# Layer 3's slots: the front's pieces in other steps of a batch

## What is computed

```python
# attention branch, heads of 8 channels
q, k, v = split(x @ qkv_w.T + qkv_b)
k, v = layernorm(k), layernorm(v)              # over the 8 channels of a head
kv = einsum('bhqd,bhqe->bhde', k, v) / Q * temperature + attn_bias
att = einsum('bhqd,bhde->bhqe', q, kv) + x
y1 = gelu(att @ p1_w.T + p1_b) @ p2_w.T + p2_b + x
# feed-forward branch, soft mixture of 16 experts with 64 slots each
x = layernorm(x); se = layernorm(slot_embeds) * scale
logits = einsum('bnd,esd->bnes', x, se)
dispatch = softmax(logits, axis=1)             # over the tokens
slots = einsum('bnd,bnes->besd', x, dispatch)
```

## Time and profile before

| what | value |
|---|---|
| median of 3 runs | 2108.69 us (2106.41 to 2111.24) |
| the profiled execution, in all | 2109.77 us |
| its span | 2107.9 us |
| mean granted TensorE clock | 0.965 |
| TensorE matmul busy, whole span | 1911.7 us (91%) |
| VectorE / ScalarE / GpSimd busy | 1685.2 (80%) / 1469.3 (70%) / 1214.1 us (58%) |
| stage of the slots | about 1674 to 1895 us |

### The profile page before, as it was taken

The page is one execution under the profiler, slowest core; times in us unless marked ns, Lnnn a source line. Parts: engine busy times, 40 slices in busy tenths (PEclk is TensorE's granted clock), DMA queues, the critical chain, the costliest instruction groups (busy, mean ns, idle before and its releaser), DMA issues.

```text
span 2107.9 us, 38803 instructions
## 1 busy us (share of the span) xinstructions
PE 1911.7 (91%) x13494; PEld 1464.8 (69%) x13494; DVE 1685.2 (80%) x3903; ACT 1469.3 (70%) x2914; POOL 1214.1 (58%) x1026
## 2 busy tenths in 40 slices
PE   4899999999999998687986999999999888889998
PEld 3667676767667676554683888888887666668797
DVE  7899999989898998377197888888888787764686
ACT  5788888888878788154235767777777777776575
POOL 3878888787878875167062555555555554437300
PEclk7999999999999999599998999999999999999999
DMA  6999898899989884201000000000001000012000
GB/s 189 340 311 319 287 321 282 312 306 310 313 286 319 285 300 172 91 1 39 1 1 6 1 1 1 1 1 1 1 1 32 0 1 1 1 34 87 11 2 41
DMA packets 72264, 263.99 MB, mean 125 GB/s; under 512 B 10822, under 2 KB 30406, under 8 KB 71558
## 3 DMA queue, kind: packets, MB, share of 16 engines
q1 hardware_dynamic: 71126, 256.53, 35.8%
q10 hardware_dynamic: 944, 4.98, 0.6%
HBM read 140.17 MB, written 121.31 MB: 124 GB/s over the span
## 4 chain that ended last, share of the span: by engine, by line
PE 41%; ACT 7%; DVE 6%; POOL 1%; issue 1%; DVEq 0%; ACTq 0%; POOLq 0%
PE PS L157 11%; PE PS L161 8%; PE PS L335 8%; PE PS L163 8%; PE PS L162 7%; ACT AR L167 3%; ACT L167 1%; DVE DR L181 1%; DVE AR L185 1%; ACT PT L171 1%; DVE PT L181 1%; POOL AR L176 1%; DVE AR L181 1%; DVE AR L193 1%; ACT AR L171 1%
## 5 line engine op out<-in xcount | busy, mean ns | idle before, releaser
L167 ACT ACTIVATE AR<-PS,AR 128x512 f32<-128x512 f32 x1024 | 697.7, 689 | 213.5 <-DVE AR L193 105.4
L193 DVE TENSOR_REDUCE AR<-PS 128x1 f32<-128x512 f32 x896 | 615.2, 687 | 92.5 <-PE PS L163 77.3
L335 PE MATMUL PS<-ident,AR 128*128 128x128 f32 x3816 | 582.0, 277 | 30.0 <-DVE PT L181 15.0
L157 PE MATMUL PS<-AR 128*128 128x128 bf16 (+7 forms) x4126 | 488.7, 358 | 53.1 <-DVE AR L1375 14.2
L335 PEld LDWEIGHTS PS<-ident,AR 128*128 128x128 f32 x3816 | 444.0, 142 | 123.7 <-issue 42.9
L181 POOL TENSOR_TENSOR AR<-AR 128x512 f32<-128x512 f32 (+6 forms) x325 | 389.1, 1216 | 208.0 <-DVE AR L181 91.4
L176 POOL TENSOR_SCALAR AR<-AR 128x512 f32<-128x512 f32 (+1 forms) x146 | 252.8, 1732 | 272.3 <-DVE AR L1743 203.7
L171 ACT ACTIVATE AR<-PS 128x512 f32<-128x512 f32 (+3 forms) x596 | 346.6, 586 | 80.5 <-PE PS L335 46.4
L157 PEld LDWEIGHTS PS<-AR 128*128 128x128 bf16 (+4 forms) x4126 | 290.9, 131 | 134.5 <-issue 61.7
L171 ACT ACTIVATE PT<-PS 128x512 fp32r<-128x512 f32 x320 | 191.3, 598 | 165.1 <-PE PS L335 130.5
L181 DVE TENSOR_TENSOR AR<-PS,AR 128x512 f32<-128x512 f32 (+3 forms) x321 | 211.5, 659 | 69.9 <-PE PS L157 58.0
(11 more groups left out here) (175 smaller groups left out, 2958.8 us busy)
## 6 DMA issues: line engine op xcount, KB each, us to landing
scr<-AR SPq DMA_DIRECT2D x128, 800.0 KB, 4.4
XN<-scr SPq DMA_DIRECT2D x85, 768.0 KB, 6.4
AR<-scr SPq DMA_DIRECT2D x43, 768.0 KB, 6.5
AR<-qsc SPq DMA_DIRECT2D x96, 192.0 KB
qsc<-AR SPq DMA_DIRECT2D x16, 384.0 KB, 4.0
qsc<-AR SPq DMA_DIRECT2D x16, 256.0 KB, 4.5
AR<-in_wgu SPq DMA_DIRECT2D x16, 256.0 KB, 3.1
qsc<-AR SPq DMA_DIRECT2D x16, 128.0 KB, 3.9
```

The lines of the kernel that those rows point to most:

```text
L157: return pe.e.matmul(out, lhsT, rhs, start=start, stop=stop)
L167: return ac.e.activation(out, in_, func, bias=bias, scale=scale, accum_out=accum)
L193: return dv.e.tensor_reduce(out, in_, AX.X, ALU.max, negate=True)
L335: return pe.e.transpose(out, in_, ident[0:k, 0:k])
```

## The change

Only the four tables of steps change. Their values become tuples, so that a step may hold two pieces of one entry, and `in_order` reads them so. The inputs' tables (I_PE, I_DV, I_AC, I_PO) stay.

```diff
-        F_PE = {1: "tr", 3: "kv0", 4: "q", 5: "kv1", 13: "km", 15: "kq", 23: "p1", 26: "p2"}
-        F_DV = {2: "z", 4: "kv0", 6: "kv1", 8: "v1", 10: "vn", 14: "km", 16: "ta", 27: "x2"}
-        F_AC = {2: "hi", 5: "qt", 7: "sq", 9: "root", 10: "xnh", 24: "gelu"}
+        F_PE = {2: ("tr",), 4: ("kv0",), 6: ("q", "kv1"), 16: ("km",), 20: ("kq",), 23: ("p1",), 26: ("p2",)}
+        F_DV = {3: ("z",), 5: ("kv0",), 7: ("kv1",), 10: ("v1",), 12: ("vn",), 17: ("km",), 21: ("ta",), 27: ("x2",)}
+        F_AC = {3: ("hi",), 7: ("qt",), 9: ("sq",), 11: ("root",), 12: ("xnh",), 24: ("gelu",)}
         AMID = ("qt", "root")
-        F_PO = {3: "lo", 5: "pb", 11: "gb", 13: "polo"}
+        F_PO = {5: ("lo",), 7: ("pb",), 12: ("gb",), 14: ("polo",)}
...
-            at = {u: [(pieces[u - 8 * b], b) for b in range(NB) if u - 8 * b in pieces] + ([(inputs[u], 0)] if u in inputs else [])
+            at = {u: [(what, b) for b in range(NB) for what in pieces.get(u - 8 * b, ())] + ([(inputs[u], 0)] if u in inputs else [])
                   for u in range(-PRE3, STEPS3)}
```

## The result

The changed kernel takes 2139.39 us (median; 2138.69 to 2140.00) against 2109.97 us for the kernel before on the same chip: ratio 1.0136, 95% interval 1.0121 to 1.0151, so 29.4 us slower. The forecast was 2128.0 us, slower, with a range of 2110 to 2138. The result lies 1.4 us above that range. The direction and the wait that carried the forecast were right; the size was short by some 10 us, most of what the runs can account for being a cost of TensorE's clock that the forecast put at nothing.

What follows compares the result with a forecast made beforehand. Bound: ScalarE's 13.4 us block, `z` and `lo`, then four TensorE steps. Start-up 1.0, five batches 16.7, last batch 0.4 and drain 1.2 sum to 19.3 us, taking 2108.69 to 2128.0 us; range 2110 to 2138.

Steps and rivals of the forecast that it cites:

- One load more per batch, six times: ScalarE: 4 table loads a batch instead of 3, in 6 batches, 7.7 us of ScalarE; whether it shows depends on place.
- Step 3: TensorE's pv waits for ScalarE's slot copy behind the root, starting 6.15 us after step 2's last matmul (R); idle 5.0 us.
- Step 6: TensorE starts at 14.3 instead of 12.4 after R, as GpSimd's gb holds up VectorE's `norm`: 1.9 us.
- The batch: One batch of layer 3's slots takes 29.75 us instead of 26.42: 3.33 more, five times 16.7.
- Steps 7 and 2: TensorE's small waits: 0.5 us before step 7's pv, 0.6 us before step 2's scores, for ScalarE.
- The clock: TensorE at half clock for about 3.2 us on steps 4 to 5 behind the idle; counted as 0, hidden by VectorE's chain.
- The rival: Slower still by the clock: half clock not hidden, 1.6 us a batch, 8 in all, total 2140; chance 0.13.
- Start-up: Stretch before the first full batch: u = 24 starts 0.3 us later, 1 us with the held `norm` of u = 21; counted 1.0.
- Drain: End of the stage behind the last batch: 1.2 us more; the experts' later weight transfer costs nothing.
- The table serves both: Rival: the logarithm's table also serves exp, step 3 is 2.56 shorter, batch 27.2 us, 2115; chance 0.14 with the side-waits rival.
- Faster: Rival: splitting ScalarE's block frees TensorE; batch 25 us, 2102, or 2087 with all waits hidden; chance 0.07.
- No change: the side waits vanish: Rival: gb's hold, the qt and the exp load hide; batch 26.4 us, 2111; chance 0.14 with the table rival.

Runs made afterwards that it cites:

- e5: Changed kernel with the root in step 5 (r = 13) instead of step 3, vn and gb at 14, km at 17 and 18: 2100.39 us, ratio 0.9946.
- e1: Changed kernel with ScalarE's slot copy issued right behind step 3's `hi`, ahead of the root: 2139.57 us, ratio 1.0135.
- e9: Changed kernel with 40 extra transposes of the identity on TensorE ahead of the pv that waits behind the root: 2133.87 us, ratio 1.0103.
- e11: The kernel before, unchanged, profiled and timed once more: 2111.70 us, ratio 1.0003.
- e8: The changed kernel, unaltered, profiled and timed a second time: 2139.40 us, ratio 1.0132.
- e10: Changed kernel with entry 0's front pieces left in the steps of the kernel before, entries 1 to 7 as changed: 2136.34 us, ratio 1.0111.
- e2: Changed kernel with the root's logarithm replaced by an exponential, so no table load is left in the root: 2113.64 us, ratio 1.0014.
- e6: Kernel before with only the k-and-v chain (root, vn, gb, km, kq and others) moved, inputs and projections left: 2108.82 us, ratio 0.9988.

## Why the prediction was right and where it fell short

- **One load more per batch, six times:** right. From 1674 us on there are 31 loads instead of 25. Worked out as a cost it was rightly not counted by itself: e5 has the same 31 and is faster than the kernel before.
- **Step 3, the step that carried the forecast:** right to 0.1 us (pv at R + 6.25 for 6.15, wait 4.60 for 5.0). e1 confirms that `lo` for the next transposes is late by the same amount. The reading of the earlier trace rows was loose: of the 14.0 us only 12.3 stand before the scores (five waits of 2.46), the rest before pv.
- **Step 6:** right. At full clock (e9) it starts at R + 14.36 for 14.3, waiting 1.78 us for 1.9, and `norm` takes 1.53 us under gb. VectorE and GpSimd, the changed kernel:

```profile
1808.70 1.53 DVE L176 TENSOR_SCALAR AR<-AR 128x512 f32<-128x512 f32 x1
```

```profile
1807.60 4.90 POOL L181 TENSOR_TENSOR AR<-AR 128x1024 f32<-128x1024 f32 x2 [14.14 <-DVE AR L181]
```

  The Trainium skill's "SBUF — State Buffer" (SBUF: two separate sides) has whichever of the two engines starts first hold the shared port pair for its whole instruction. These rows agree, as do the 2.12 us of the start-up and the 2.37 of the last batch: each of these `norm`s ends 0.3 us behind the end of the gb instruction in which it was issued (1810.23 here, against 1807.60 + 2.35).
- **The batch:** 29.94 us at full clock for a forecast of 29.75. The 26.42 from which it was subtracted is not at full clock, though: it is the mean over four batches of 26.43 to 26.58, with 3.4 us at half clock in each, and one of 26.04 without. The earlier trace rows are all from that one. In e11 too the one batch at 1.00 takes 26.04, the others 26.34 to 26.57. At full clock on both sides the change costs 3.9 us a batch, not 3.5. Steps 7 and 2 have the small waits that the text gave them (0.19 and 0.30 for 0.5; 0.31 for 0.6).
- **The clock, the step that failed:** "I take 0 of it, as VectorE's chain to step 6 is 1.9 us longer than TensorE's". The cover was real and of that size (1.78), but the stretch at half clock was sized from one behind an idle of 2.5 us (put at 3.2 us, by the reading above 3.4) and is 6.8 us behind 4.6 in eight of the ten batches of the two profiles. The five batches pay 1.1 us for it in the first profile (150.81 less e9's 149.72) and 3.3 in the second (153.06). The last batch was not looked at for it and pays 2.2 (26.46 less 24.30), since `norm` slips behind the start of gb's second instruction; that is all but 0.2 of what the forecast missed there: without it the last batch is 0.6 longer than before, for 0.4. Together 3.2 to 5.5 us; e9's timing says 5.5. By the second profiles (e8 and e11) the stage is 27.5 us longer, 8.2 more than the forecast's 19.3: 5.5 of it is the clock, 1.3 the start-up, 1.1 the batches at full clock, 0.6 the last batch, and the drain gives back 0.3. The rival gave 8 for the batches and had a chance of 0.13, yet the range ended short of it.
- **Start-up:** mis-sized too, 3.1 us for 1.0. "There is no row for this mixture" was true; the row that came near, gb's hold on `norm`, I had counted once at u = 21 and not for the first root, where layer 2's sums are in VectorE's queue. e10 takes 2.3 of the 3.1 away. e11, the kernel before again, has 66.3 us for this stretch instead of 65.4, so about 1 us of it is chance.
- **Drain:** 0.9 for 1.2; the experts' first matmul waits 1.20 us for GpSimd, 1.18 in e11, so the later transfer of their weights shows nowhere.
- **The rivals.** "The table serves both" is out: two loads stand around each logarithm, and their loss is what e2 shows. "Faster" is out for this placing, but its core, that splitting the block frees TensorE, holds in e5. It said that the case decides by whether the slot copy of step 3 is done within 1.1 us of R; e5's pv at R + 3.0 with a gain shows that bound to have been too strict. "No change: the side waits vanish" is out: step 6's 1.78 us and `norm`'s hold are there in every batch.
- **What stays open.** The stage is 25.4 us longer in the first profiles and 27.5 in the second ones (265.9 less 238.5). The medians differ by 29.4 us in the result, where the kernel before has four times from 2106.4 to 2116.5, and by 27.3 beside e8 (2139.40 less 2112.15, of 19 times), which the second profiles' stage covers. In what is left of the first difference, up to 4 us, no instruction differs, and no run here settles what it is.

## What to carry to other kernels

When a long block moves on one in-order engine, list everything that this engine issues behind it in the same step, and place it where none of that is what the bottleneck engine needs next: with the root in step 3 this change cost 29 us, with it in step 5, km one step later, it gained 12 (e5). Two moves that are harmless alone can put a consumer behind the block (here the input `hi`), so cost the combination, not the parts. An idle stretch of the matmul engine has a second price, slower matmuls behind it; look for cover in every place where it occurs, the last batch too. There a slip of 0.92 us became 2.45, as it pushed an instruction behind another engine's. And before subtracting a cycle built from rows from a measured mean, see whether the rows and the mean have the same granted clock.

## What the runs showed of the hardware

- Table loads: 1283 ns each, and the next instruction starts 0.01 us behind (1798.74 + 1.28 against 1800.03), as behind 30 of the changed kernel's 31. The drain of 1380 ns that "ScalarE: Activation LUTs" (What ACT_TABLE_LOAD costs) of the Trainium skill adds is not seen: two loads less shorten the wait by 2.69 us (e2), not by 5.3.
- TensorE idle for 4.6 us in one piece is followed by 3.4 us at 1.2 GHz (two batches of the changed kernel) or 6.8 (its other three and all five of e8). An idle of 2.5 us is followed by 3.4 us in eight of ten batches of the kernel before (both profiles) and by none in two, one of 1.9 us by 3.4 in all five of e2. In e6, with waits of 1.73 and 1.50 us and 2.2 us of work between them, the granted clock stays at 1.00 in the second to fifth batch; in e5, with a longest wait of 1.35, in all five. 40 transposes of constant data in the idle stretch keep it at 1.00 (e9) and are worth 5.5 us.
- A GpSimd tensor-tensor over 128x1024 (2.45 us) makes VectorE's 0.47 us `norm` last from 0.84 to 2.37 us, the longer the sooner behind its start it is issued, while VectorE's instructions on PSUM beside it keep their 0.68 us.
